# Attention values by seven block products instead of eight, turned in two groups, one step behind the scores

## What is computed

```python
q = (inputs_q @ Wq).reshape(b, sq, H, HD) * (1.0 / np.sqrt(HD))
k = (inputs_kv @ Wk).reshape(b, skv, H, HD)
v = (inputs_kv @ Wv).reshape(b, skv, H, HD)
scores = jnp.einsum('bqhd,bkhd->bhqk', q, k)
attn = jax.nn.softmax(scores, axis=-1)
ctx = jnp.einsum('bhqk,bkhd->bqhd', attn, v).reshape(b, sq, H * HD)
return ctx @ Wo
```

## Time and profile before

| | before |
|---|---|
| median of 3 runs | 2122.44 us (2121.5 to 2127.71) |
| the profiled execution | 2124.15 us, span 2122.3 us |
| PE, share of the span | 97% |
| DVE | 55% |
| ACT | 43% |
| GpSimd (POOL) | 7% |
| mean granted TensorE clock | 0.989 of 2.4 GHz |

### The profile page before, as it was taken

How to read it: one execution, slowest core, us unless ns; L and a number is a source line. 1 busy time by engine, 2 the same in 40 slices (tenths; PEclk the granted TensorE clock), 3 DMA queues, 4 the chain that set the end, 5 groups by cost and what they waited for, 6 DMA issues and landing times.

```text
span 2122.3 us, 30139 instructions
## 1 busy us (share of the span) xinstructions
PE 2054.2 (97%) x11196; PEld 1108.1 (52%) x11200; DVE 1161.2 (55%) x2703; ACT 910.0 (43%) x1985; POOL 154.4 (7%) x209
## 2 busy tenths in 40 slices
PE   5899999999999999999999999999999999999886
PEld 5655555555555555555555555555555555555562
DVE  5664545555555546566666565455555555554426
ACT  3444545444445344344444444444444444443312
POOL 1100101000000101000001001010000010000001
PEclk8999999999999999999999999999999999999998
DMA  5433544444535345464544453343433443532660
GB/s 165 120 69 77 110 88 112 91 102 97 106 84 114 71 94 113 94 129 90 118 104 110 103 112 71 84 90 66 99 72 84 80 86 69 98 63 52 191 218 5
DMA packets 516705, 206.79 MB, mean 97 GB/s; under 512 B 418864, under 2 KB 502832, under 8 KB 515664
## 3 DMA queue, kind: packets, MB, share of 16 engines
q1 hardware_dynamic: 516560, 204.88, 43.4%
HBM read 97.59 MB, written 4.46 MB: 48 GB/s over the span
## 4 chain that ended last, share of the span: by engine, by line
PE 93%; DVE 4%; issue 1%; ACT 1%; DMA 1%; POOL 0%; DVEq 0%; SPq 0%; POOLq 0%; ACTq 0%
PE ps_s L1119 24%; PE ps_t L1119 18%; PE ps_c L1143 12%; PE ps_b L1143 12%; PE ps_a L1143 12%; PE ps_u L1143 12%; PE ps_b L1097 1%; DVE bulk L777 1%; PE ps_t L1201 1%; DMA bulk<-in_vo 1%; PE ps_s L1080 0%; PE ps_c L1108 0%; PE ps_s L1244 0%; PE ps_b L1108 0%; PE ps_u L1268 0%
## 5 line engine op out<-in xcount | busy, mean ns | idle before, releaser
L1119 PE MATMUL ps_s<-bulk 128*128 128x384 f16 (+2 forms) x3264 | 579.0, 321 | 23.3 <-DVE bulk L777 23.2
L1119 PE MATMUL ps_t<-bulk 128*128 128x384 f16 (+2 forms) x2448 | 450.0, 320 | 1.5 <-ACT ps_t L630 1.0
L1119 PEld LDWEIGHTS ps_s<-bulk 128*128 128x128 f16 x3264 | 315.6, 99 | 237.0 <-DVE bulk L777 26.2
L1119 PEld LDWEIGHTS ps_t<-bulk 128*128 128x128 f16 x2448 | 235.6, 98 | 151.4 <-ACT ps_t L630 1.9
L630 ACT ACTIVATE ps_t<-ps_s 128x384 f32<-128x384 f32 (+2 forms) x136 | 62.9, 462 | 583.4 <-PE ps_s L1119 583.4
L1143 PE MATMUL ps_u<-nring,pt 128*128 128x512 f16 x1194 | 269.1, 379 | 0.0
L1143 PE MATMUL ps_a<-nring,pt 128*128 128x512 f16 x1194 | 269.1, 379 | 0.0
L500 POOL TENSOR_TENSOR stages<-stages 128x256 f32<-128x256 f32 x196 | 146.0, 745 | 1677.3 <-DMA stages<-in_ctx 1658.8
L1143 PE MATMUL ps_b<-nring,pt 128*128 128x512 f16 x1158 | 260.7, 379 | 0.0
L1143 PE MATMUL ps_c<-nring,pt 128*128 128x512 f16 x1158 | 260.7, 379 | 0.0
L823 DVE SCALAR_TENSOR_TENSOR pp<-prob,pp 128x768 f16<-128x768 f32 (+2 forms) x272 | 239.7, 923 | 0.0
(11 more groups left out here) (200 smaller groups left out, 1677.7 us busy)
## 6 DMA issues: line engine op xcount, KB each, us to landing
stages<-in_ctx SPq DMA_DIRECT2D x392, 128.0 KB, 2.8
wst<-in_w SPq DMA_DIRECT2D x64, 256.0 KB, 3.4
bulk<-in_vo SPq DMA_DIRECT2D x16, 512.0 KB, 4.9
acc<-in_qk SPq DMA_DIRECT2D x12, 512.0 KB, 5.0
pt<-pp SPq DMA_TRANSPOSE x272, 4.0
tern_d<-wter SPq DMA_DIRECT2D x32, 128.0 KB, 3.0
bulk<-tern_d SPq DMA_DIRECT2D x2, 2048.0 KB, 11.6
wst<-in_qk SPq DMA_DIRECT2D x4, 512.0 KB, 5.9
```

The source lines that it names most:

```text
L1119: ins = mm(out, q_part(e, qlo, a)[:, c * P:(c + 1) * P], t_moving(k, tlo, b, c), start=(first and c == 0 and qlo == 0 and tlo == 0), stop= ...
```

## The change

The value product takes the same seven-product form as the scores. The two heads' probabilities are one block matrix (rows: heads; columns: halves of each chunk), the context another (columns: halves of the 512). A step of three chunks now has 7 products of 9 matmuls, each 256 columns wide: 63 instead of 36 matmuls of 512.

- GpSimd makes the sums of the probability blocks (`sum_p`: four operations of `cols(k)` columns a step) and the sums of the value side of a chunk (`sum_t` for every load, no longer only for those of the scores).
- The high and low parts are written for seven blocks instead of four, in five pieces (`hi_part`, `lo_part`), after the exponentials of the same step. DVE's low parts stand behind `split_lo` and the new sum `value_sum_d` of the step.
- `pt` has one set instead of two. The turns are two groups of 8 and 6 times `cols(k)` columns (before: twice 4 times), and wait for the last value product of the step before (`v4_done`).
- The values run one step behind the scores (`LAG` = 1), in one set of PSUM banks, with three ACT copies (`value_a`, `value_e_u`) and two DVE sums (`value_sum_d`, `value_sum_e`) in between.
- The value part of a chunk is split as seven blocks (1792 columns) instead of four (1024).
- The queries' low part is made a step earlier. Weights are quantized in every second step of 64 instead of in each of 32. The scale of the probabilities is half as large. Small buffers share space with larger ones; the masks and gate weights are loaded near the end of the steps, x a second time, and the last attention weight earlier.

```diff
-LAG = 2
+LAG = 1
...
             def turn_p(k, g):
-                sp.wait_ge(lo_done[g], k + 1)
-                if k >= LAG:
-                    sp.wait_ge(u_done[g], k - 1)
-                n = 4 * cols(k)
-                at = ((k % 2) * 2 + g) * 4 * WIN * P
+                sp.wait_ge(lo_done, 5 * k + (2, 5)[g])
+                if k:
+                    sp.wait_ge(v4_done, k)
+                at, n = p_at(k, g), (8, 6)[g] * cols(k)
...
+            def sum_p(k):
+                for n, (dst, a, b, op) in enumerate(((S1, A21, A22, ALU.add), (S3, A11, A21, ALU.subtract),
+                                                     (S2, S1, A11, ALU.subtract), (S4, A12, S2, ALU.subtract))):
...
+                    nc.gpsimd.tensor_tensor(prob_part(k, dst), prob_part(k, a), prob_part(k, b), op).then_inc(p_sum, 1)
+            for k in range(NS):
+                found = prep_at(k)
+                if found is not None:
+                    sum_t(found[0])
+                sum_p(k)
...
             def exp_head(k, g):
                 h = heads_of(k)[g]
                 act.wait_ge(nm_done[g], k + 1)
                 if k:
-                    act.wait_ge(lo_done[g], k)
+                    act.wait_ge(lo_done, 5 * k)
+                    act.wait_ge(p_sum, 4 * k)
...
+            def value_a(k):
+                act.wait_ge(v1_done, k + 1)
...
+                nc.scalar.activation(val_b, val_a, ACT.Copy).then_inc(va_copied, 1)
...
                 exp_head(k, 0)
+                if k:
+                    value_a(k - 1)
                 exp_head(k, 1)
-                if k + 1 < NP:
-                    q_hi_part(k + 1)
+                if k:
+                    value_e_u(k - 1)
...
-                for g in range(2):
...
-                    nc.scalar.activation(pp_part(k, g, 0), prob_of(k, g), ACT.Copy, scale=P_SCALE).then_inc(hi_done[g], 1)
+                hi_part(k, A22, 3, 0)
+                hi_part(k, S1, 1, 1)
+                hi_part(k, S3, 1, 2)
+                hi_part(k, S2, 1, 3)
+                hi_part(k, S4, 1, 4)
+                if ii < NP:
+                    q_hi_part(ii)
...
+            def value_sum_d(k):
+                v.wait_ge(v7_done, k + 1)
+                v.wait_ge(ve_copied, k + 1)
...
+                nc.vector.tensor_tensor(val_d, val_b, part_e[:, 0:BLK], ALU.add).then_inc(vd_done, 1)
...
             def step(k):
-                if k:
-                    lo_head(k - 1, 0)
-                    lo_head(k - 1, 1)
                 v.wait_ge(s2_done, k + 1)
                 max_head(k, 0)
...
                 split_lo(k)
...
-                add_values(k - LAG, 0)
-                add_values(k - LAG, 1)
...
-                if 0 <= k - QUANT_AT < 2 * WP:
-                    quant(k - QUANT_AT)
+                if 0 <= k - QUANT_AT < 4 * WP and (k - QUANT_AT) % 2 == 0:
+                    quant((k - QUANT_AT) // 2)
+                if k:
+                    value_sum_d(k - 1)
+                lo_part(k, A22, 3, 1)
+                lo_part(k, S1, 1, 2)
+                lo_part(k, S3, 1, 3)
+                lo_part(k, S2, 1, 4)
+                lo_part(k, S4, 1, 5)
...
+                if k:
+                    value_sum_e(k - 1)
+                add_values(k - 1, 1)
+                add_values(k - 1, 0)
...
+            def values(k):
+                _, lowest, w = STEPS[k]
+                pe.wait_ge(in_pt[0], 16 * (k + 1))
...
+                value_product(k, val_a, A11, B11, True, False).then_inc(v1_done, 1)
...
+                value_product(k, val_e, S1, T1, True, False).then_inc(v5_done, 1)
+                pe.wait_ge(in_pt[1], 16 * (k + 1))
+                pe.wait_ge(va_copied, k + 1)
+                value_product(k, val_b, S2, T2, False, False).then_inc(v6_done, 1)
+                value_product(k, val_a, A12, B21, False, True)
+                pe.wait_ge(vu_copied, k + 1)
+                value_product(k, val_b, S3, T3, False, False).then_inc(v7_done, 1)
+                pe.wait_ge(ve_copied, k + 1)
+                value_product(k, val_e, S4, B22, False, True).then_inc(v3_done, 1)
+                pe.wait_ge(vd_done, k + 1)
+                value_product(k, val_b, A22, T4, False, True).then_inc(v4_done, 1)
```

More of the change, by code:

```diff
@@ L247, in bank_d, with row_of @@
             return ps_t[:, D:D + cols(k)]
[L249 to L255, removed]
+        def row_of(g):
+            return (ps_w, ps_v)[g][:, D - BLK:D + BLK]
         def heads_of(k):
@@ L317, in perceiver_layer @@
         al_done = sem("al_done")
-        hi_done = [sem(f"hi_done{g}") for g in range(2)]
-        lo_done = [sem(f"lo_done{g}") for g in range(2)]
-        u_done = [sem(f"u_done{g}") for g in range(2)]
+        hi_done = sem("hi_done")
+        lo_done = sem("lo_done")
+        p_sum = sem("p_sum")
+        v1_done = sem("v1_done")
+        v5_done = sem("v5_done")
+        v6_done = sem("v6_done")
+        v7_done = sem("v7_done")
+        v3_done = sem("v3_done")
+        v4_done = sem("v4_done")
+        va_copied = sem("va_copied")
+        ve_copied = sem("ve_copied")
+        vu_copied = sem("vu_copied")
+        vd_done = sem("vd_done")
+        ve_done = sem("ve_done")
+        in_xr = sem("in_xr")
         r_done = sem("r_done")
@@ L674, in _ @@
                                      ACT.Copy).then_inc(ut_cp, 1)
+                if f == 0:
+                    value_a(NS - 1)
+                    value_e_u(NS - 1)
                 if f == 6:
@@ L906, in _ @@
             q_four_sums(1)
-            split_lo(-1, (1, 1, 0, 1))
+            split_lo(-1, (1, 1, 0))
+            q_lo_part(1)
             for k in range(NS):
                 step(k)
-            lo_head(NS - 1, 0)
-            lo_head(NS - 1, 1)
             sums(NS - 1)
-            add_values(NS - 2, 0)
-            add_values(NS - 2, 1)
+            v.wait_ge(lo_done, 5 * NS)
             def norm_head(f):
@@ L937, in _ @@
             o_copy(0)
+            value_sum_d(NS - 1)
+            value_sum_e(NS - 1)
+            add_values(NS - 1, 1)
             add_values(NS - 1, 0)
-            add_values(NS - 1, 1)
             norm_head(2)
@@ L1149, in step, with value_product @@
-            def step(k, between=None):
+            def value_product(k, dst, a, b, first, last):
+                _, lowest, w = STEPS[k]
+                g = a // PURE
+                for n in range(w):
+                    c = next(c for c in range(lowest, lowest + w) if ring_slot(c) == window(k)[4][n])
+                    for plo, clo in ((0, 0), (0, 1), (1, 0)):
+                        tile = p_at(k, g, plo, a % PURE) + n * P
+                        ins = mm(dst, pt[:, tile:tile + P], n_part(c, clo, b), start=(first and n == 0 and plo == 0 and clo == 0),
+                                 stop=(last and n == w - 1 and plo == 1), skip_group_check=True)
+                return ins
@@ L1150, in step @@
+            def step(k):
                 _, a, w = STEPS[k]
@@ L1182, in _ @@
                 step(k)
-            for g, n in chunks(NS - 2):
-                values(NS - 2, g, n)
             def turn(f):
@@ L1213, in _ @@
             finish(0)
-            for g, n in chunks(NS - 1):
-                values(NS - 1, g, n)
+            values(NS - 1)
             for f in range(1, H):
```

335 lines of the change are left out of this document (181 added, 154 removed).

## The result

The changed kernel takes 2273.48 us (median of four runs, 2270.56 to 2277.84); the kernel before, on the same chip, 2125.07. The ratio is 1.0700, 95% interval 1.0670 to 1.0731: 7% slower. The forecast was 2205 in a range of 2030 to 2260. The direction is right; the loss is +148 us against +84.

A forecast was written before the change was run, and what follows sets the result against it. PE bounded the kernel before; afterwards DVE's loop, contended by GpSimd, at 15.2 us a step. (15.2 - 14.604) x 124 = +74, start +8, end +2: +84, so 2206 against 2122.44 (likeliest 2205), range 2030 to 2260.

The forecast's parts named there:

- PE's own work, 13.70: PE's matmuls in a full step after the change: 13.70 us, 0.90 less than before, -112 us over 124 steps.
- DVE's loop without contention, 12.4: DVE's in-order list tied to PE in a loop: 12.4 us a step without contention, below PE's 13.70.
- Contention, +2.9: DVE's two-input passes and GpSimd's sums exclude each other: low parts 2.9 us late, loop 15.3 with split and chunk sums.
- the three kinds: Full steps by chunk work: split and chunk sums 15.3 us, split only 14.2, chunk sums only 14.5; mean 14.8.
- the 0.4 for `quant` and passed-on delay: Added to the mean 14.8 for quantizing passes meeting GpSimd and delay passed between steps: 0.4 us a step, 15.2 used.
- The unknown price of 384 columns on GpSimd: GpSimd's sum of 384 columns, not in the trace: taken as 1.0 us, between 0.745 and 1.12.
- The turns, "hidden": Turning DMAs into the one `pt` set: pair about 8.3 us, loop 13.6, landing near +16.4 and hidden in the contended step.
- Start, +8: First seven steps: DVE gets more work, the earlier query low part gives most of it back; +8 us (-15 to +25).
- End, +2: Last steps of one or two chunks: less PE work covers the longer path from exponential to turned blocks; +2 us.
- The turns bind: Rival: with 9 us for the pair of turns the loop is 14.3 us, -37 us, near 2085; chance 0.10.
- The cover holds: Rival: DVE and GpSimd passes slip past each other, step 13.8 us, -100 us, time 2023; chance 0.20.

The follow-up runs named there:

- experiment 8: Changed kernel with low parts written from one SBUF input and half of the tiles turned, both from step 10 on; output not whole: 2103.14 us.
- experiment 10: Kernel of experiment 9 with half of the tiles turned from step 10 on; output not whole: 2053.20 us.
- experiment 1: Changed kernel with DVE's low parts written from one SBUF input instead of two from step 10 on; output differs: 2155.16 us.
- experiment 3: Changed kernel with a wait in GpSimd's list, so the chunk sums run after the step's low parts; output whole: 2191.47 us, ratio 1.0301.
- experiment 4: Changed kernel with GpSimd's four probability sums covering 16 columns instead of 384 from step 10 on; 2189.81 us.
- experiment 2: Changed kernel with half of the tiles turned from step 10 on, the other blocks keeping old contents; 2242.86 us.
- experiment 6: Changed kernel with the queries' low part written behind the two `add_values` in the first steps; output whole: 2260.37 us, ratio 1.0632.
- experiment 7: Changed kernel with the edits of experiment 5 and experiment 6, and the reduction three steps later; output whole: 2128.14 us, ratio 1.0004.
- experiment 5: Changed kernel with experiment 3's wait and, from step 10 on, the four probability sums on DVE instead of GpSimd; output whole: 2134.26 us.
- experiment 9: Experiment 7 with the three quantizing passes moved from DVE to GpSimd, behind the low parts; output whole: 2105.26 us, ratio 0.9906.

## Why the prediction came out as it did

*PE's own work, 13.70.* Right. 0.109 a matmul of 256 columns, and steps of 13.70 in experiments 8 and 10. The steps of 13.95 there are a term that the forecast put at nothing: ACT's copy `value_a`. It stands behind the exponentials of head 0, and the third value product waits for it. In 64 of the 124 steps these exponentials are two instructions a head and not one. Experiment 10, first a step of 13.70, then one of 13.95 (L693 is the copy):

```profile
297.61 0.37 ACT L693 ACTIVATE ps_w<-ps_v 128x256 f32<-128x256 f32 x1
298.28 1.15 PE L1255 MATMUL ps_w<-nring,pt 128*128 128x256 f16 x9
...
325.58 0.38 ACT L693 ACTIVATE ps_w<-ps_v 128x256 f32<-128x256 f32 x1
326.10 1.14 PE L1255 MATMUL ps_w<-nring,pt 128*128 128x256 f16 x9
```

The two value products before it began at 296.31 and 323.88. In the first step the third follows after PE's own 1.97, the copy done in time; in the second it starts 0.14 behind the copy's end, after 2.22. That is the 0.25.

*DVE's loop without contention, 12.4.* Not seen by itself. That it is below PE's pace is shown by experiment 8, where 46 steps are at 13.70 with the same passes in DVE's list, the low parts of 384 columns at 0.55.

*Contention, +2.9.* The mechanism is right (experiments 1, 3, 4). Low parts beside four chunk sums took 5.36 and 5.06 against 3.22, +2.1 and +1.8, where I had four meetings at 0.52, +2.1; in steps without chunk sums 3.69 and 3.89, one meeting. The size is right also for the whole: with the turns halved a step takes 15.27, and 15.17 without the 12 us of the reduction, against 15.2. Part of that closeness is luck. Counted as in the forecast, from the end of one last score product to the next, the steps of experiment 2 that don't quantize take 15.4 (forecast 15.3), 14.2 (14.2) and 15.05 (14.5) for the three kinds: 15.0 in the mean instead of 14.8, while the 0.4 for `quant` and passed-on delay was too much. The unknown price of 384 columns on GpSimd, taken as 1.0, measured 0.99 to 1.00 alone (1031.51 in the changed kernel: 0.99). The estimate by the Trainium skill (GPSIMD Engine Reference, "Elementwise — side-by-side cycle accounting") was the same (384 columns on the line from 256 in 0.745 to its 2,048 in 4.497 are 1.01), and the trace agrees with it. `quant` was priced as three more such meetings, and its passes did go from 1.34 to 3.43; I had not noticed that these have only one SBUF input. The rule of the Trainium skill that I cited (SBUF — State Buffer, "Who interferes with whom", a two-input instruction of DVE contends) doesn't cover them, but the same section does: it says that a `tensor_scalar` can enter a mode that takes both port pairs, and contend then, except in the form that also writes out its accumulator. The traces agree: `quant`'s passes are such `tensor_scalar`s, do 512 columns in 0.43 where a low part of 384 takes 0.55, and are held up; experiment 1's low parts write out a running sum and are not. As a whole `quant` costs less than forecast: where its steps lie (50 to 113, every second one) a step takes 15.63 in the mean against 15.30 of those before (steps 9 to 48 without the long one), 0.17 a step of all 124.

*The turns, "hidden".* This is the step of the working that failed: 0.25 of the 0.32 us that a step is above the forecast, 31 us of the 68 that the whole is (experiment 2). The lengths in it were near (24 tiles in 5.6, the pair in 8.4 for 8.3 forecast). But I let the second turn begin when its low parts were ready, at +11.7, and land at +16.4, with 1.6 between the two issues from a pair of 12 tiles each. Counted from 998.36, where the last score product ends, the low parts were done at +12.4 and the first turn was issued at +9.9; with 24 tiles its issue holds the queue for 3.8 us, so the second began at 1012.04, +13.7, and landed 4.6 later, at +18.3. PE could have used it at +18.1. In this step the copy `value_a` ended 0.06 behind the turn and is named as what PE waited for; in the next step, and in one elsewhere, it is the turn, with 0.54 and 0.60. Over the whole run PE waits 44.5 us for `pt` in front of `ps_w` products. Some turns are slow besides: the second one of the step before, issued at 995.36, was 6.4 us on its way, which is the gap of 1.37.

```profile
829.12 1.05 PE L1224 MATMUL ps_w<-nring,pt 128*128 128x256 f16 x8 [0.60 <-DMA pt<-pp]
...
1016.83 1.14 PE L1224 MATMUL ps_w<-nring,pt 128*128 128x256 f16 x9 [0.17 <-ACT ps_w L675]
...
1032.33 1.16 PE L1224 MATMUL ps_w<-nring,pt 128*128 128x256 f16 x9 [0.54 <-DMA pt<-pp]
```

Before, with the values two steps behind, no value matmul of the full steps waited for a turned block.

*A step unseen: the reduction.* 12 us, the other 0.10 a step. GpSimd's list had slack of 31 us at that place; the change gives every step a use for GpSimd, and I listed the sums it adds, not the one long thing already in its list.

*Start, +8.* +28.5, the second largest miss. Contention with chunk sums is 11 us of it (experiment 3) and the query's low half in front of `add_values` 12 (experiment 6), which I had taken as a gain. (In the four runs whose edit works from step 10 on, step 7 begins at 155.0 to 157.1, so a difference of a few us would say nothing here.) With both edits (and the sums still on GpSimd there) step 7 is at 137.3, still 12.5 behind; that rest was not taken apart. I looked at what the move takes off L777's waits, and not at who stands behind L846 in DVE's list: the two `add_values`, for which PE waits to begin the next query.

*End, +2.* +9.8. With the edits of experiment 7 it is +4.6 (2123.9 less 1932.7, against 186.6), with the turns halved (experiment 2) +3.7. So contention and turns may both have a part; they were not taken apart further.

*The rivals.* "The turns bind" was wrong as the bound, but the turns weigh: 0.25 to 0.37 us a step. "The cover holds" fell: DVE and GpSimd did not slip past each other by themselves. The edits of experiments 3 and 5 together made them, and there the mean step is 14.49, under the 14.60 of before but far from the rival's 13.8, since the turns were not hidden and DVE had the sums to do. Measured terms in the forecast's form: (15.52 - 14.60) x 124 = +114, +28.5, +9.8: +152 on the span, +148 in the medians.

## What to carry to other kernels

Before a pass goes to a half-idle engine, ask which passes of its neighbour it will stand beside, and give it a wait that puts it elsewhere: one such wait was worth 82 us here. Before the idle time of an engine or a queue is spent, walk its list for the rare long entry (a reduction of 13 us, a turn that lands 1.6 us late), and count a transfer's time of issue as well as its landing, since that idle time was their cover. Of the 112 us that PE gave up in the sum, the best whole kernel keeps 21: what the neighbours' lists hold decides the rest.

## What the runs showed of the hardware

- A float32 pass with one SBUF input on DVE (`quant`'s, 512 columns, 0.43 to 0.48 alone) takes 1.0 to 1.1 in the mean beside GpSimd's sums of 384 columns (changed kernel, experiments 1 and 3), and 0.43 to 0.48 again where these sums are cut to 16 columns (experiment 4). Low parts with one input (experiment 1) beside chunk sums stay at 547 ns. The two differ in their speed (512 columns in 0.43, 384 in 0.55) and in what they write (in place or to bfloat16, against float16 with a running sum); a kernel in which only one of these differs was not run. GpSimd's instruction is the same kind in both.
- A sum on GpSimd takes 0.22 with 16 columns, 0.46 with 128, 0.73 with 256 and 1.00 with 384 (medians where DVE is idle; the 16 from experiment 4, the others from the changed kernel): some 0.2, and 0.27 for each 128 columns.
- A turn of 24 tiles holds SyncE's queue 3.66 us, one of 18 tiles 2.74, one of 12 1.45 (medians); they land 5.6, 4.7 and 3.7 us after their issue.
- Slow turns come together with a transfer of the queue that the page lists as "q8 instruction", 16 KB every 17 to 19 us. In the changed kernel, steps 11 to 130, the 33 turns with such a transfer between issue and landing land after 6.41 (24 tiles) and 6.28 (18 tiles) in the median, the other 207 after 5.62 and 4.65. In experiment 7 the 43 with one land after 7.27 and 6.27, the other 197 after 5.62 and 4.65. In both kernels this falls on the first turn of steps 16, 22, 28, 34, 40 and 46: it goes by steps, not by time. That one causes the other is not shown.
- The three quantizing passes take 0.48, 0.43 and 0.43 on DVE, and 0.69, 1.93 and 1.67 on GpSimd (experiment 9).
